# Rounding back and row shift: from GpSimd to ScalarE, between attention and gate/up

## The reference

```
x = layernorm(x + attention(x, wq, wk, wv, wo))             # 32 query heads, 8 key/value heads, window 128
x = layernorm(x + matmul(fake_quant(x), fake_quant(ctx)))   # per batch: 512x1024 by 1024x1024
x = layernorm(x + ffn(x))                                   # silu(gate) * up, rounded towards zero, then down

fake_quant(x, scale, zp):  q = clip(round(x / scale + zp), 0, 255);  return (q - zp) * scale
```

## Time and profile before

| | |
|---|---|
| three runs | 1550.97, 1550.74, 1546.24 us (median 1550.74) |
| the profiled execution | 1546.86 us, its span 1545.10 us |
| busy in the span | PE 96%, PEld 79%, DVE 62%, ACT 51%, POOL 55% |
| the chain that ended last | PE 85%, DVE 6%, ACT 4%, issue 2%, DMA 1%, POOL 1% |

### The profile page before, as it was taken

How to read it: one execution, slowest core, us unless ns; L and a number is a source line. 1 busy time by engine, 2 the same in 40 slices (tenths; PEclk the granted TensorE clock), 3 DMA queues, 4 the chain that set the end, 5 groups by cost and what they waited for, 6 DMA issues and landing times.

```text
span 1545.1 us, 23314 instructions
## 1 busy us (share of the span) xinstructions
PE 1484.5 (96%) x7516; PEld 1215.4 (79%) x7533; DVE 963.9 (62%) x1505; ACT 785.7 (51%) x1572; POOL 851.3 (55%) x753
## 2 busy tenths in 40 slices
PE   7899999999999999999999999998799999999796
PEld 6788888888888788888888888875478888887443
DVE  7644444444346566666666666668667777767597
ACT  5433333333344455454545454625766676666564
POOL 4577777776455454545545455435677667666000
PEclk9999999999999999999999999999899999999998
DMA  6377777775324533424252333402023232332111
GB/s 218 142 275 275 273 278 277 278 274 209 130 102 154 212 114 125 149 75 149 68 173 93 131 119 123 162 3 81 16 69 121 82 122 98 106 121 83 55 41 70
DMA packets 83477, 218.14 MB, mean 141 GB/s; under 512 B 8416, under 2 KB 8800, under 8 KB 83424
## 3 DMA queue, kind: packets, MB, share of 16 engines
q1 hardware_dynamic: 83424, 217.48, 40.0%
HBM read 153.49 MB, written 63.96 MB: 141 GB/s over the span
## 4 chain that ended last, share of the span: by engine, by line
PE 85%; DVE 6%; ACT 4%; issue 2%; DMA 1%; POOL 1%; SPq 1%; ACTq 0%; DVEq 0%; POOLq 0%
PE ps L813 9%; PE ps L815 9%; PE ps L814 9%; PE ps L1044 8%; PE ps L1045 8%; PE ps L881 7%; PE ps L882 7%; PE ps L883 7%; PE ps L1072 5%; PE ps L863 2%; PE ps L833 2%; PE ps L864 2%; PE ps L834 2%; PE ps L832 2%; PE ps L845 2%
## 5 line engine op out<-in xcount | busy, mean ns | idle before, releaser
L1044 PE MATMUL ps<-xt_h,w_h 128*128 128x512 f32 x704 | 276.8, 393 | 5.9 <-ACT w_h L1412 5.9
L1045 PE MATMUL ps<-xt_l,w_h 128*128 128x512 f32 x704 | 275.7, 392 | 0.0
L813 PE MATMUL ps<-xo_h,wb_h 128*128 128x512 f32 x644 | 252.1, 391 | 7.0 <-issue 6.1
L814 PE MATMUL ps<-xo_l,wb_h 128*128 128x512 f32 x644 | 251.5, 391 | 0.0
L815 PE MATMUL ps<-xo_h,wb_l 128*128 128x512 f32 x644 | 251.5, 391 | 0.0
L1719 POOL TENSOR_TENSOR pm_l<-pt_l,upto 128x512 fp32r<-128x512 f32 x64 | 83.1, 1299 | 250.7 <-DVE pt_l L1974 250.7
L881 PE MATMUL ps<-wo_h,o_h 128*128 128x512 f32 x512 | 206.5, 403 | 1.2 <-DMA wo_l<-wo_low 0.9
L882 PE MATMUL ps<-wo_l,o_h 128*128 128x512 f32 x512 | 199.8, 390 | 0.0
L883 PE MATMUL ps<-wo_h,o_l 128*128 128x512 f32 x512 | 199.6, 390 | 0.0
L1044 PEld LDWEIGHTS ps<-xt_h,w_h 128*128 128x128 f32 x704 | 133.3, 189 | 35.1 <-ACT w_h L1412 3.9
L1688 POOL TENSOR_TENSOR wb_l<-wf_l,wb_h 128x512 fp32r<-128x512 f32 x69 | 90.0, 1304 | 128.2 <-ACT wb_h L1184 64.3
(11 more groups left out here) (185 smaller groups left out, 3349.8 us busy)
## 6 DMA issues: line engine op xcount, KB each, us to landing
raw<-w_att SPq DMA_DIRECT2D x47, 512.0 KB, 5.4
wp_raw<-w_att SPq DMA_DIRECT2D x32, 512.0 KB, 5.8
wo_high<-wp_h SPq DMA_DIRECT2D x32, 512.0 KB, 2.8
wo_low<-wp_l SPq DMA_DIRECT2D x32, 512.0 KB, 4.1
q_rows<-c SPq DMA_DIRECT2D x64, 256.0 KB, 2.5
q_raw<-q_rows SPq DMA_DIRECT2D x64, 256.0 KB, 2.6
wo_h<-wo_high SPq DMA_DIRECT2D x16, 1024.0 KB, 5.2
wo_l<-wo_low SPq DMA_DIRECT2D x16, 1024.0 KB, 7.4
```

The costliest lines, as they stand in the source:

```text
L813: pe.matmul(prod_ps[i], wh, chunk(xo_h[i], c), start=(i in OPENS and c == 0), stop=False, skip_group_check=True)
L814: pe.matmul(prod_ps[i], wh, chunk(xo_l[i], c), start=False, stop=False, skip_group_check=True)
L1044: pe.matmul(dst, w, xt_h[:, c, rows], start=(c == 0), stop=False)
L1045: last = pe.matmul(dst, w, xt_l[:, c, rows], start=False, stop=(c == DC - 1))
```

## The change

Two functions come into ScalarE's part, `quantise_rows` and `move_rows`, and the same work leaves GpSimd's. The semaphores, buffers and everything on the other engines stay.

```diff
+            def quantise_rows(t):
+                act.wait_ge(x_rounded, t + 1)
+                if t == 0:
+                    act.wait_ge(sizes_ready, 1)
+                wait(act, xq_turned, t - 1)
+                act.activation(x_q[:, t % 2, :], x_scaled[:, t % 2, :], ACT.Identity,
+                               bias=param(UNROUND)).then_inc(x_quant, 1)
+
+            def move_rows(t):
+                act.wait_ge(shift_ready, t + 1)
+                act.wait_ge(x1_columns, t + 1)
+                act.activation(resid[:, t, :], resid[:, t, :], ACT.Identity, bias=shift[:, t % 2, :]).then_inc(x1_moved, 1)
...
             def slot(i):
                 if 4 <= i < TILES + 4:
                     root(1, i - 4)
+                if 2 <= i < TILES + 2:
+                    quantise_rows(i - 2)
                 if 1 <= i < TILES + 1:
                     normed(0, i - 1)
...
                 if 2 <= i < TILES + 2:
                     copy_turned(i - 2)
+                if 3 <= i < TILES + 3:
+                    move_rows(i - 3)
                 if 5 <= i < TILES + 5:
                     columns_whole(i - 5)
...
-                pool.tensor_scalar(x_q[:, t % 2, :], x_scaled[:, t % 2, :], 1.0, -(ROUND + CENTRE), ALU.mult,
-                                   ALU.add).then_inc(x_quant, 1)
...
-                if 3 <= i < TILES + 3:
-                    t = i - 3
-
-                    pool.wait_ge(shift_ready, t + 1)
-                    pool.wait_ge(x1_columns, t + 1)
-                    pool.tensor_scalar(resid[:, t, :], resid[:, t, :], 1.0, shift[:, t % 2, :], ALU.mult,
-                                       ALU.add).then_inc(x1_moved, 1)
...
-            for i in range(4, max(LOW_BY_POOL + 6, TILES + 3)):
-                if i < TILES + 2:
-                    quantise_rows(i - 2)
+            for i in range(2, max(LOW_BY_POOL + 6, TILES + 2)):
                 slot(i)
```

## The result

| | before | changed |
|---|---|---|
| median | 1547.51 us of 6 runs (1546.24 to 1550.97) | 1556.65 us of 6 runs (1553.74 to 1560.35) |
| the profiled execution's span | 1545.1 us | 1552.8 us |

The account below looks back on a forecast made before the run. Bound: a ring of ScalarE up to x_whole, two GpSimd operations holding VectorE's links, and some VectorE time. Row shift 4.2, slot 9 2.3 and slot 4 1.0 sum to +7.5 us on 1550.7: 1558.2 us, range 1550.5 to 1562.5.

Parts of the forecast that it names:

- The row shift: Slots 5 to 8, between x_qt and x_whole: delays x_whole and GpSimd's two operations by 1.04 us a slot, +4.2 us.
- Slot 4: TensorE's turn of tile 2 waits for x_q, now behind root(1,0): +1.0 us, bounds 0 and 2.3.
- Slot 9: Tile 7's rounding back stands behind two w_h and root, so TensorE waits for x_q: +2.3 us.
- Covered, without anything to spare: Slots 6 to 8: late x_q delays cross, but cross_done comes at 1091.5 to 1093.1 against the shift's end at 1093.0; no cost.
- the sign that I gave: Expected in the trace: VectorE's cross_add starting right behind the row shift.
- the hole that made the rounding back free: ScalarE's idle time between root(1) and normed(0), slots 6 to 8: rounding back fits with 0.3 us to spare, costing ScalarE nothing.
- Rival C: Longer slots bring cross to TensorE's low clock: 3.2 in the slots plus 1.8 at cross(6), 5 us more, 1563; 7 in 100.
- It moves as a whole: Behind the stage, from the last tile's x_whole to the w_h TensorE awaits: everything hangs on that x_whole, so nothing is given back.
- Rival A: No measurable change: ScalarE's 10.8 us idle of 39 absorbs slot 4 and half of slot 9, 1555; 12 in 100.
- the ring: Each 10.25 us slot: ScalarE to the end of x_whole 5.26 us, two GpSimd operations 4.7, about 0.25 of VectorE.
- Rival B: Faster: VectorE's L2138 and L2143 no longer held by GpSimd's port use, 6.3 us gained, 1544.4; 4 in 100.
- Rival D: Slots 1 to 4: GpSimd's addition takes the port first, VectorE's L2150 waits 2.4 us; 1560 to 1562; 5 in 100.

Follow-up runs that it names:

- its filled kernel: Kernel with only the rounding back on ScalarE, plus unread TensorE products ahead of the turn and behind cross in slots 6 to 9: 1547.72 us, ratio 1.0001.
- both filled kernels: Unread TensorE products in slots 6 to 9, added to the kernel with only the rounding back moved (ratio 1.0001) and to the changed kernel (1.0039).
- filled, the changed kernel: Changed kernel plus unread TensorE products, nine ahead of the turn and six behind cross, slots 6 to 9: 1552.85 us, ratio 1.0039 to before.
- the filled kernel above: Kernel before with xt_l on VectorE, plus ten unread TensorE products behind cross in slots 6 to 8: 1542.13 us, ratio 0.9967 to before.
- the kernel with the last rounding early: Changed kernel with only tile 7's rounding back moved, to right before the two w_h rows: 1550.37 us, ratio 1.0026 to before.

## Why the prediction was right, and where its working failed

Slower by 9.1 us against the +7.5 that I forecast; the median of before came out 3.2 us lower with more runs, so 1556.65 stands against 1558.2. On the two spans it is +7.7 us. That this is so near to 7.5 is in part luck: my three terms came to 7.1 us, two that I had put at nothing came to 1.14 (cross(6) at a lower clock) and 0.94 (behind the stage), and 1.48 ahead of and behind all this went the other way unexplained. The upper bounds of my terms add up to 12.2 us, too, and not to the 11 that I wrote.

- **The row shift, +4.2.** Measured +3.90 alone, and 2.87 + 1.04 = 3.91 in the changed kernel. Right, by the mechanism given.
- **Slot 4, +1.0.** The turn of tile 2 is 0.92 us late and waits 0.47 for x_q; right. With the rounding back alone that turn is 0.30 us late (0.34 up to slot 8 in its filled kernel), and with the row shift alone not at all, so the rest needs the row shift ahead of cross_add, as the step said.
- **Slot 9, +2.3.** 2.27 us beside the fourth row shift, and the same in both filled kernels; right. In the kernel with the rounding back alone it is 3.14.
- **"Covered, without anything to spare".** This step failed. I let cross_done come with the row shift's end at the latest and so priced the late x_q at nothing in slots 6 to 8. In the changed kernel cross ends 0.4 us behind the shift in slot 7 (1095.27 against 1094.90) and 1.1 in slot 6 (1084.70 against 1083.62). So the sign that I gave, cross_add right behind the shift, did not come. What still covers it is that the first link comes before xt_l has ended, with little to spare in slot 6: L2134 there is held for no more than 0.06 us (0.26 instead of about 0.20). Nor had I seen what follows once it is not covered. Then the first link is held by the addition, root(1) and the x_q behind it come after the addition's end, and the hole that made the rounding back free is gone, because root(1) was early only as long as xt_l and not the addition held that link. With both moves this is hidden, with the rounding back alone it makes slots of 12.2 us. For that run I had said +2.3 to +2.8 us; it cost 7.0.
- **Rival C, the clock.** Half true. Its share at cross(6), 1.8 us, is there with 1.14. Its share in the slots, 0.8 each, is not: filled, the changed kernel has the same slots. That GpSimd's cover of a late cross has an end was right in kind, and the rounding back alone passes it; but past it the cost comes as one step and not in proportion.
- **"It moves as a whole".** Nearly: 0.94 us more come between the first gate/up product and the late w_h. This stretch takes 37.11 to 37.29 us in every kernel with the row shift on ScalarE and xt_l on GpSimd, the one with the shift alone included (37.13), and 36.15 to 36.22 in before and in every kernel with the shift on GpSimd and xt_l there too. The last x_whole does not move in it (18.62 us behind that product before, 18.56 after), so not all hangs on that. What moves is GpSimd: in slot 10 the row shift stands ahead of x_whole, the xt_l made from it starts 1.0 us later, and with it all that GpSimd does next. A later VectorE operation, u_round, is then 1.5 us long instead of 0.41, in all six kernels of the first kind and in none of the second. It looks like one more hold, but no experiment took it apart. Before, then after with GpSimd's row beside it:

```profile
1138.62 0.41 DVE L2255 TENSOR_SCALAR u_round<-u_size 128x512 f32<-128x512 f32 x1
```

```profile
1144.92 2.13 POOL L1818 TENSOR_TENSOR resid<-u_again,resid 128x512 f32<-128x512 f32 x1
...
1145.83 1.51 DVE L2251 TENSOR_SCALAR u_round<-u_size 128x512 f32<-128x512 f32 x1
```

- **Rival A (no change).** The idle share of ScalarE, 10.8 us, was real and did not help: the row shift stood in the ring, and the hole's price was its place.
- **Rival B (faster by a freed port).** As expected, the links stayed held by the two operations that stayed. Taking one of them away (xt_l on VectorE) gives 5.0 us of the rival's 6.3; halving the addition on before, 4.2.
- **Rival D (VectorE's rounding held by the addition).** In slots 1 to 4 the two do start together, but VectorE first, by 0.04 to 0.05 us, and its 0.69 us stay. The hold fell on GpSimd, whose addition took 2.90 us. VectorE's row and GpSimd's row at that place in slot 1 of the changed kernel:

```profile
1036.50 0.69 DVE L2146 TENSOR_SCALAR x_scaled<-x_scaled 128x1024 f32<-128x1024 f32 x1 [0.96 <-ACT x_scaled L1381]
```

```profile
1036.55 2.90 POOL L1802 TENSOR_TENSOR resid<-resid,ctx_sum 128x1024 f32<-128x1024 f32 x1 [10.12 <-ACT x_scaled L1381]
```

What stays open: why cross took 5.2 to 5.5 us in slots 6 and 7 of the changed kernel and 5.4 to 6.1 with the rounding back alone; the 1.4 us by which the medians differ more (9.1) than the spans of the two profiled executions (7.7), which is within how far single runs differ, and which now and then a slot like the 13.26 us above would also explain, though no trace of the changed kernel shows one; and the 1.6 us of the filled kernel above.

## What to carry to other kernels

An operation moved to an idle engine costs what its place in that engine's queue makes late. The same eight rows of 1.14 us cost nothing at the end of the slots and 7 us a few rows on, behind root(1), which waits for the statistics of a product that the row's own result feeds. So follow every ring that runs through the new place, also the ones with slack today, and take TensorE's share of a ring at the granted clock of that stretch and not at full clock. Where a small operation takes over a microsecond, look at its port neighbour's rows first: moving the neighbour was worth 5 us here, while moving the two operations around it cost 9.1.

## What the hardware showed that I had not expected

- Unread products made a kernel faster: 54 of them in slots 6 to 9 brought the granted clock from 1072 to 1104 us from 0.78 to 1.00 and took the ratio from 1.0045 to 1.0001.
- GpSimd's addition takes 2.35 us, and 2.90 where VectorE's one-input operation on 128x1024 began 0.05 us ahead of it. So the hold went in both directions here, and showed as a long duration of the held row, not as idle time before it (a link of about 0.20 us was recorded at up to 2.33). The Trainium skill (SBUF — State Buffer, "Who interferes with whom") counts such a one-input form among those that can take the shared pair; the 0.55 us more agree with that.
- Between two GpSimd operations that followed each other a waiting link of VectorE got through: in the changed kernel L2134 waited during xt_l, ended at 1098.27, and the addition began at 1098.20. In the kernel with the last rounding early the same link came 0.02 us after the addition's start and took 2.33 us.
